# First feed-forward of a four-part network on eight cores: constants, halo and W1 sums at the start, rounding and clipping of the ternary weights, places for W2's pieces

## What is computed

```
def weight_quant(w):                       # for W1 and W2, each 4096 x 1024
    scale = 1.0 / clip(mean(abs(w)), 1e-05)
    return clip(round(w * scale), -1, 1) / scale
def act_quant(x):                          # per token
    scale = 127.0 / clip(max(abs(x), axis=-1), 1e-05)
    return clip(round(x * scale), -128, 127) / scale
h = act_quant(layernorm(x)) @ weight_quant(w1).T
h = silu(depthwise_conv1d(h, conv_w, conv_b))      # three taps along the tokens
x = x + 0.5 * act_quant(h) @ weight_quant(w2).T
```

## Time and profile before

| | us |
|---|---|
| profiled execution, time | 3381.05 |
| its span (core 3, the slowest) | 3379.4 |
| other cores' spans | 3299.0 to 3374.5 |
| median of 3 runs | 3529.73 (3400.16 to 3662.04) |
| TensorE / VectorE / ScalarE busy | 2719.5 / 1984.2 / 1703.0 |
| first feed-forward | about 0 to 865 |

### The profile page before, as it was taken

One profiled execution on the slowest core, in us unless ns is written; L12 is line 12 of the kernel. 1 busy time (PEld: TensorE's weight loads), 2 busy tenths in 40 slices (PEclk: granted clock), 3 DMA queues, 4 the chain that ended last, 5 costly groups with the idle time before them and its releaser, 6 DMA issues.

```text
span 3379.4 us, 39052 instructions; the slowest of 8 cores (3299.0 to 3379.4 us)
## 1 busy us (share of the span) xinstructions
PE 2719.5 (80%) x11770; PEld 1162.0 (34%) x11770; DVE 1984.2 (59%) x2842; ACT 1703.0 (50%) x2015; POOL 382.7 (11%) x437
## 2 busy tenths in 40 slices
PE   1355768799489999999999883678879959889789
PEld 0122223344133444444433331333334424334334
DVE  1477667775557777777765124677777514443433
ACT  2776656563423666666654623666656313414430
POOL 0000102112310001110000100001211211211310
PEclk7676889899798999999965796889989979999999
DMA  7343533233612022220110154122323360000001
GB/s 228 111 122 121 173 123 125 87 96 103 149 19 45 22 39 57 42 39 19 30 35 7 38 148 142 35 83 86 123 83 92 103 212 1 1 20 31 1 7 69
DMA packets 153945, 259.11 MB, mean 77 GB/s; under 512 B 37968, under 2 KB 74064, under 8 KB 153424
## 3 DMA queue, kind: packets, MB, share of 16 engines
q1 hardware_dynamic: 121312, 199.77, 19.4%
q0 software_dynamic: 32432, 56.83, 7.0%
HBM read 220.70 MB, written 52.56 MB: 81 GB/s over the span
## 4 chain that ended last, share of the span: by engine, by line
PE 61%; DVE 14%; ACT 9%; issue 8%; DMA 7%; POOL 1%; SPq 1%; DVEq 0%; ACTq 0%; POOLq 0%
PE fb L1099 11%; PE fb L869 8%; PE aups L1556 8%; PE apps L1670 7%; PE asps L1651 7%; PE mb L2169 6%; PE ajps L1520 3%; DVE fbig L910 2%; PE rs L2060 2%; DVE amx L1567 2%; ACT fbig L905 2%; PE mb L2224 2%; PE mb L1968 1%; DMA xbd<-alnb 1%; DMA fbig<-w1h 1%
## 5 line engine op out<-in xcount | busy, mean ns | idle before, releaser
L1567 DVE TENSOR_REDUCE amx<-aups 128x1 f32<-128x512 f32 x1024 | 662.6, 686 | 253.8 <-PE aups L1556 251.9
L1660 ACT ACTIVATE aet<-asps 128x1024 bf16<-128x1024 f32 x512 | 521.6, 1025 | 294.0 <-PE asps L1651 290.3
L869 PE MATMUL fb<-fxsc,fw1r 128*128 128x512 bf16 x2048 | 561.1, 415 | 96.4 <-DVE fbig L914 66.1
L1099 PE MATMUL fb<-fbig 128*128 128x512 bf16 x2048 | 504.1, 396 | 95.5 <-DVE fbig L839 53.8
L1556 PE MATMUL aups<-ahd 65*128 65x512 bf16 x1024 | 381.0, 415 | 22.1 <-DVE amx L1567 8.5
L1670 PE MATMUL apps<-aet,avt 128*65 128x512 bf16 x1024 | 339.8, 416 | 16.4 <-ACT aet L1660 11.0
L869 PEld LDWEIGHTS fb<-fxsc,fw1r 128*128 128x128 fp8e4 x2048 | 213.3, 105 | 400.6 <-issue 209.3
L1651 PE MATMUL asps<-ahd 65*128 65x512 bf16 x1024 | 340.0, 417 | 0.0
L1099 PEld LDWEIGHTS fb<-fbig 128*128 128x128 fp8e4 x2048 | 204.8, 101 | 362.2 <-issue 143.1
L910 DVE SCALAR_TENSOR_TENSOR fbig<-fb,cw2sb,fbig 128x511 f32<-128x511 f32 x256 | 191.3, 747 | 213.0 <-ACT fbig L905 210.8
L905 ACT ACTIVATE fbig<-fb,cbsb,cw2sb 128x512 f32<-128x512 f32 x256 | 196.3, 770 | 234.4 <-PE fb L869 222.0
(11 more groups left out here) (249 smaller groups left out, 2968.7 us busy)
## 6 DMA issues: line engine op xcount, KB each, us to landing
fw1r<-wq SPq DMA_DIRECT2D x224, 128.0 KB, 2.1
fbig<-wq SPq DMA_DIRECT2D x112, 256.0 KB, 2.7
fbig<-w1h SPq DMA_DIRECT2D x32, 512.0 KB, 12.9
fw2f<-w2h SPq DMA_DIRECT2D x64, 256.0 KB, 3.1
fbig<-w2h SPq DMA_DIRECT2D x28, 512.0 KB, 3.9
fxq<-x SPq DMA_DIRECT2D x8, 1024.0 KB, 9.0
fbig<-x POOLq DMA_DIRECT2D x32, 256.0 KB, 5.6
xa<-fbig POOLq DMA_DIRECT2D x32, 256.0 KB, 3.7
```

The source lines that it names most:

```text
L869: tp = T(lambda e, dc=dc: e.matmul(bank[b][:, :], sl[:, o + dc * 128:o + (dc + 1) * 128], xr[:, dc * 512:(dc + 1) * 512], start=(dc == 0), ...
L1099: tp = T(lambda e, j=j: e.matmul(bank[2 + j][:, :], w2r[s][:, o + j * 128:o + (j + 1) * 128], xi2[:, hc * 512:(hc + 1) * 512], start=(hc = ...
L1567: lambda e, hh=hh, c=c: e.tensor_reduce(m[:, c:c + 1], ups[hh][:, :], axis=AX.X, op=ALU.max),
L1660: ta = A(lambda e: e.activation(et[g % 3][:, :], sps[s][:, :], AF.Exp, scale=0.125), wait=[tp, tk.get(("ef", g % 3))])
```

## The change

1. The constants `ones_bf` and `ones_f` are dropped; the other eight are issued on GpSimd's queue, one behind the other without waits in between, and the four compute engines wait for all of them. The `barrier()` ahead of the first feed-forward goes.
2. Start: the order is x, `xh`, all 32 chunks of W1, two of W2. The layer norm of quarter 0 is emitted by its step list, one step behind each chunk's sum, and `halo`, now a generator with a yield after each dependent stage, behind it in the same way. Sums of even chunks are on ScalarE, of odd ones on VectorE.
3. Pass 0: `w1_quant` becomes `w1_round` (hc + 5) and `w1_clip` (hc + 4).
4. W2's mean moves from ahead of pass 1 to behind its first two W1 items. W2's pieces get eight places (four in `w2f`, the four of `res`); rounding is 8 iterations ahead, clipping 7, the load 15.
5. For quarter 0, `evict_sum` does scale and addition of x on VectorE, inside PSUM and into `ev`; x is loaded into `ev`, since `res` holds pieces.

The diff, cut to its core:

```diff
-        dma(CHX, ident_bf[:, :], identbf_in.ap())
...
-        const_tag = dma(CHX, bo_sb[:, :], bo_in.ap())
+        for dst, src in ((ones_k, onesk_in), (ident_f, identf_in),
+                         (ones_sq, onesq_in), (cw_sb, cw_in),
+                         (cb_sb, cb_in), (ident_bf, identbf_in),
+                         (mask_su, mask_in), (bo_sb, bo_in)):
+            const_tag = em.go("gpsimd", lambda e, d=dst, s=src:
+                              e.dma_start(d[:, :], s.ap()), dma=s_const)
...
         def ffn(x_src, x_dst, first):
-            barrier()
+            if not first:
+                barrier()
...
                 def w1_chunk_abs(k):
...
+                    if k % 2 == 0:
+                        j = (k // 2) % 2
+                        t = A(lambda e: e.activation(
+                            xsc[1][:, j * 1024:(j + 1) * 1024], c, AF.Abs,
+                            accum_out=part[:, k:k + 1]),
+                            wait=[wtok["c", k], wtok.get(("a", k - 4))])
+                    else:
+                        t = V(lambda e: e.tensor_reduce(
+                            part[:, k:k + 1], c, axis=AX.X, op=ALU.add,
+                            apply_absolute_value=True), wait=[wtok["c", k]])
...
+                def w2_place(k):
+                    i = k % 8
+                    if i < 4:
+                        return w2f[:, i * 512:(i + 1) * 512]
+                    return res[i - 4]
...
                 def w2_piece_load(k):
...
+                    w = [wtok.get(("pq", k - 8)), wtok["bd", PLAST[i]][0]]
+                    if k < 4:
+                        w += [wtok["b", 2], wtok["b", 3]]
+                    elif k < 8:
+                        w += [wtok["b", 30], wtok["b", 31]]
...
+                def evict_sum(half):
+                    for j in range(4):
+                        dc = half * 4 + j
+                        t = V(lambda e, j=j: e.tensor_tensor(
+                            bank[2 + j][:, :], bank[2 + j][:, :],
+                            sv_bc[:, :], ALU.mult),
+                            wait=[qtok["o", j], ch["svbc"]])
...
+                        t = V(lambda e, j=j: e.tensor_tensor(
+                            ev[j], bank[2 + j][:, :], ev[j], ALU.add),
+                            wait=[t, rest[j]])
+                        free[2 + j] = [t]
+                        evfree[j] = dget(
+                            s_ev[j], x_dst[dc * 128:(dc + 1) * 128, 0:QT],
+                            ev[j], wait=[t], eng="gpsimd")
...
                 if first:
-                    ln_load(0)
-                    for k in range(4):
-                        w1_chunk_load(k)
...
+                    steps = ln_steps(0)
+                    steps.pop(0)()
+                    edge_steps = halo()
+                    next(edge_steps)
+                    for k in range(HC):
                         w1_chunk_load(k)
+                    w2_abs(0)
+                    w2_abs(1)
+                    steps.pop(0)()
+                    for k in range(HC):
                         w1_chunk_abs(k)
+                        if steps:
+                            steps.pop(0)()
+                        else:
+                            next(edge_steps, 0)
...
-                    if first and hc + 4 < HC:
-                        w1_quant(hc + 4)
-                        w2_abs(hc + 4)
+                    if first:
+                        w1_round(hc + 5)
+                        w1_clip(hc + 4)
+                        if hc + 4 < HC:
+                            w2_abs(hc + 4)
...
-                        if gen and it + 4 < 64:
-                            w2_quant(it + 4)
-                            if it + 8 < 64:
-                                w2_piece_load(it + 8)
+                        if gen:
+                            w2_round(it + 8)
+                            w2_clip(it + 7)
+                            w2_piece_load(it + 15)
```

More of the change, by code:

```diff
@@ L678, in halo @@
                         wait=[tc])
+                    yield
                     tp = T(lambda e: e.transpose(
@@ L749, in w1_chunk_abs @@
                 def w1_chunk_abs(k):
[L750 to L755, removed]
+                    c = big[:, k * 1024:(k + 1) * 1024]
+                    if k % 2 == 0:
[4 more added lines that the diff above has]
+                            wait=[wtok["c", k], wtok.get(("a", k - 4))])
+                        ln["xscfree"][1] = t
+                    else:
+                        t = V(lambda e: e.tensor_reduce(
+                            part[:, k:k + 1], c, axis=AX.X, op=ALU.add,
+                            apply_absolute_value=True), wait=[wtok["c", k]])
+                    wtok["a", k] = t
                 w1slot = {}
@@ L798, in w2_abs @@
                         sl = w2f[:, i * 1024:(i + 1) * 1024]
-                        w = [wtok.get(("b", k - 2)), wtok["a", 31]]
+                        w = [wtok.get(("b", k - 2)), wtok["c", 24 + i]]
                     else:
@@ L825, in w2_piece_load @@
                     wtok["pd", k] = dget(
-                        s_wf[2 + i], w2f[:, i * 512:(i + 1) * 512],
+                        s_wf[PSEM[i]], w2_place(k),
                         w2h.ap()[:, hc, half * 4:(half + 1) * 4, :]
[L828 to L835, removed]
+                        .rearrange("p a b -> p (a b)"), wait=w)
@@ L1121, in res_load @@
                         dc = half * 4 + j
-                        w = [resfree[j]]
+                        w, dst = [resfree[j]], res[j]
                         if first and q == 0:
-                            w += [wtok["b", 30], wtok["b", 31]]
-                        rest[j] = dget(s_res[j], res[j],
+                            w = [wtok["b", 30], wtok["b", 31], evfree[j]]
+                            dst = ev[j]
+                        elif first and q == 1 and half == 0:
+                            w = [wtok["pq", 60 + j]]
+                        rest[j] = dget(s_res[j], dst,
                                        x_src[dc * 128:(dc + 1) * 128,
@@ L1185, in ffn @@
                         ALU.mult), wait=[wtok["w1mean"]])
-                    for k in range(4):
-                        w1_quant(k)
-                    w2_abs(0)
-                    w2_abs(1)
+                    for k in range(5):
+                        w1_round(k)
+                        w1_clip(k - 1) if k else None
                 else:
@@ L1209, in ffn @@
                     ln_bcast()
-                    halo()
+                    for _ in halo():
+                        pass
                     ln_quant(0, 0)
@@ L1246, in ffn @@
                         if first:
-                            wtok["w2mean"] = mean_of(
-                                part[:, 32:64], 32,
-                                [wtok["b", 30], wtok["b", 31]],
-                                wst[:, 8:12], 4)
-                            wtok["w2half"] = V(lambda e: e.tensor_scalar(
-                                wst[:, 10:11], wst[:, 8:9], 0.5 / 127.0,
-                                None, ALU.mult), wait=[wtok["w2mean"]])
-                            for k in range(4):
+                            for k in range(8):
                                 w2_piece_load(k)
```

113 lines of the change are left out of this document (62 added, 51 removed).

## The result

| | before | after |
|---|---|---|
| profiled execution, us | 3381.05 | 3289.77 |
| median of 4 runs | 3464.94 (3394.69 to 3662.04) | 3301.47 (3289.77 to 3463.18) |
| after over before | | 0.9706 [0.9655, 0.9757] |

The change makes the kernel 2.9% faster, about 99 us. The forecast was 3265, a saving of 117, with a range of its own of 3230 to 3295; three of the four runs of the changed kernel lie at 3290 to 3302, mean 3298, just above that range. Between the two profiled executions the saving is 91.

What follows compares the result with a forecast made beforehand. No engine is full; a serial start and waits between engines in passes 0 and 1 bound the kernel. Savings 49 + 24 + 44 = 117 from 3381 give 3264, taken as 3265, range 3230 to 3295 (8 in 10: 3215 to 3330).

Steps and rivals of the forecast that it cites:

- A: The start, until W1's mean: constants on GpSimd's queue, earlier loads and shared sums save 49 us, between 34 and 58.
- The engines, not the loads, end last: Start: of two racing paths, the engines' path ends at 77 us and the loads' path at 68.
- 32, 16 and 13: Start, engines' path in us: 32 for the layer norm's first part, 16 for halo and quantization overlapped, 13 for sums.
- B: Pass 0 of the first feed-forward: three parts together save 24 us, between 8 and 42.
- (2): Pass 0: rounding one chunk ahead of the clip removes VectorE's 29.8 us of waits; priced at 12, from nothing to 29.8.
- (3): Pass 0: W2's mean no longer ahead of two W1 items in TensorE's queue saves 5 us.
- (1): Pass 0: W2's first two chunks asked for right behind W1's; ScalarE's 5.0 us wait goes, counted as 7.
- C: Pass 1: earlier W2 clips remove most of TensorE's waits, 47 us less 3 for x's addition on VectorE: 44.
- Only the loads pay: Rival for the first feed-forward, chance 0.22: A saves 49, B 8, C 25 less 3; 79 in all, so 3302.
- All stalls go: Rival for the first feed-forward, chance 0.12: A saves 58, B 42, C 62; 162 in all, so 3219.
- The constants are late: Rival at the start, chance 0.05: everything waits until 30 us or later for GpSimd's constant loads; saving 64, so 3317.
- Slower, by the clock: Rival for the whole kernel, chance 0.04: denser matmuls lower the granted clock; a fall of 0.064 gives about 3450.

Runs made afterwards that it cites:

- combined kernel: Changed kernel plus five edits: no constants wait on ScalarE, W2 chunks 2 and 3 at once, roundings, products and half 1's addition on GpSimd; 0.9604 over before, median 3253.01.

## Why the prediction was right and wrong

That the kernel gets faster, and in which stages, was right; the saving was forecast too large. The sum also stands on a low base, 3381.05: the lower two runs of the kernel before were 3394.69 and 3400.16, mean 3397, 16 us above it. In the later comparison, with more runs, the kernel before had a mean of 3386 (seven runs) and the changed kernel one of 3295 (four), a saving of 91. So the base accounts for 5 to 16 us of the miss, by two comparisons, and the size of the saving for 18 to 26 (117 against 99 and 91; the stages say 94 to 96). The second part is in these steps.

**A, 49 forecast, 52 measured.** Right, and the landmarks fit: first activation work at 14.2 (14), mean at 73.3 (77). "The engines, not the loads, end last" holds by about 3 us only: with loads 14.2 later the mean came 10.8 later. The terms 32, 16 and 13 of the engines' path were not tested one by one.

**B, 24 forecast, 8 to 9 measured.** The step that failed is (2), the price of rounding ahead: 12 of a range from nothing to 29.8. It is 0 within the scatter: 162.0 with the rounding back at its clip, 161.7 and 162.8 without. The prediction named the condition, "nothing if ScalarE's order is the limit", and then took a middle value. The runs don't show ScalarE alone as the limit either: work taken from VectorE was worth more (0.52) than work taken from ScalarE (0.25). What the prediction left out is in the order of the queues: both engines are equally loaded and each works in order, and VectorE meets ScalarE again at the convolution behind the clip. The mark "wait of the clip for the rounding below 10 us" was met (1.4) and was no test. (3), the mean, was right in pass 0, 5.1 for 5, but pass 1 pays 2.3 of it. That leaves 3 to 4 for (1), of 7, which was not tested apart. Pass 0 came out at 168.1 by the prediction's cut, outside its 145 to 165.

**C, 47 less 3 forecast, 39.4 less 5.7 measured.** The mechanism was right: the lead removes TensorE's waits, and that for W2's clips fell below 15 (12.7). The size was 8 high, and pass 1 stands at 172 to 175, not 168. The prediction counted 59.5 us of TensorE's waits; 5.1 more were booked on a rounding:

```profile
PE fb L1099 <- ACT fw2f L835: 5.1, 1, 5.1
```

Of these 64.6, 19.3 are left (12.7 and 6.6), and the moved mean adds 2.3. The charge for `evict_sum`, 3 of 0 to 6, was low, since pass 2 lost 5.7, and its place was wrong: at the seam, where the two-step chain delays pass 2's convolutions, which shows in 3.7 of the 5.7. So "everything after 519 the same but earlier" was wrong by the 5.7.

**The rivals.** *Only the loads pay* was right about pass 0 (8 for 9.3 measured) and wrong about pass 1 (22 for 34), and its sum, 3302, is nearest to the measured 3298 by luck, by a base that is too low: its saving of 79 is nearly as far from the stages' 94 to 96 as the forecast's 117 is. *All stalls go* failed with the first wait that moved. *The constants are late* didn't happen: they were there at 14.2, not at 30. *Slower, by the clock* didn't either: the passes that got shorter had a higher grant, 0.90 in pass 1 against 0.84 and 0.76 in pass 0 against 0.71, and the attention behind them, 1226.6 and 1223.4 against 1209.9 and 1233.6, shows no payment.

## What to carry to other kernels

A wait between two in-order engines that hand work to each other every step can be their distance and not a cost. Before pricing its removal, name the next instruction that needs the other engine; where there is one close by, as here, the price was zero. A wait of a third engine that feeds on both was different: more lead took 35 us from TensorE's waits for the clips (48.2 to 12.7) and was worth 27. Two dependent steps in place of one can cost most at the seam of two passes, where the next pass's first instructions are queued behind them: 3.7 us for four evictions here. What the other four cost in the middle of pass 1 was not measured.

## What was not expected of the hardware

The attention's time differed between executions of one program, and between the cores of one execution, and went with the granted clock. Windows of 770 to 1975 us in the changed kernel, core 2 and core 4:

```profile
770.00:1975.00 1205.00, 1080.17 (x4131) 439.05 (x4196) 763.12 (x1144) 653.66 (x730) 107.87 (x123) 0.87 0.25 55
...
770.00:1975.00 1205.00, 1031.20 (x4321) 430.47 (x4391) 796.81 (x1199) 683.95 (x769) 108.93 (x125) 0.92 0.26 58
```

In the same 1205 us core 4 at 0.92 is 190 matmuls further than core 2 at 0.87. Over all kernels run, the attention's median took 1183 to 1253 us, with nothing in it changed, so an edit worth 10 us in the first feed-forward can't be read off one execution's time, only off its stage. Why the combined kernel's attention was near the low end stays open.

Eight constants of 0.29 MB, issued by GpSimd until 5.9 us beside SyncE's loads (276 GB/s in this stage), were all there at 14.2: each took 7.1 to 8.7 us from issue to landing. One after the other on SyncE's queue, with nothing beside them, they took 1.5 to 1.8 us each. The runs don't tell the other queue's part in this from that of the loads beside it.
